# The first FFN's gating: GpSimd rounds three of four gate chunks, ScalarE scales a quarter of the sigmoids, and two loads are placed anew

## The chip, the cores and the metric

One core of a Trainium2 chip runs the whole program. The metric is the device time of one execution in microseconds (us), lower is better. The engines named here are TensorE (PE), VectorE (DVE), ScalarE (ACT), GpSimd (POOL) and SyncE (SP, which only issues DMAs); they run side by side and wait for each other by semaphores.

## The reference, cut to what matters

The program is a two-layer block over x of 16 x 256 tokens x 256 features: cross attention, a quantised gated FFN, a second cross attention, a butterfly FFN, each added to x through tanh of a gate. The change lies in the first FFN:

```python
def act_qdq(x):                        # one scale for the whole tensor
    qmax = 2.0 ** 15 - 1.0
    scale = jnp.maximum(jnp.max(jnp.abs(x)) / qmax, 1e-12)
    return jnp.clip(jnp.round(x / scale), -qmax - 1.0, qmax) * scale
...
x = act_qdq(x)                         # x is the normalised input
up = act_qdq(x @ lpbq_dequant(w_up).T)
gate = act_qdq(x @ lpbq_dequant(w_gate).T)
sig = fixed_qdq_u16(jax.nn.sigmoid(gate))    # rounded to multiples of 1/65536
gate = act_qdq(gate * sig)
o = act_qdq(gate * up)
return o @ lpbq_dequant(w_down).T
...
x = x + jnp.tanh(g_ffn[0]) * _L0_ffn_ref(_layernorm(x, axis=-1), ...)
```

Each `act_qdq` needs the maximum over all 4096 x 768 values before the first of them can be rounded. So the FFN falls into stages.

## The kernel before, in words

Everything is in `quantised_ffn` (L1463), built as three blocks one after another; in a block each engine runs its own list of instructions in order. Values lie as [128 partitions, batch pairs, 6 feature tiles (FT), tokens] in `hid`; `G` = 8 groups of 512 tokens, `GATES` = 48 tiles of 128x512.

**First block, gate products** (from 291.8 us of the span). VectorE computes x's scale, then `x_step` and `x_start` (L1667, L1668), and encodes and casts two of group 0's four tiles. ScalarE first waits for the gate value `g_in` and takes its tanh (L1788, L1789), then encodes the other two tiles and goes on to later groups (`encode`, `cast`, `turned`). TensorE transposes a group and multiplies it with the gate weights, in three passes per tile; ScalarE copies each tile to `hid` (L1808), and VectorE takes maxima and minima of two tiles at once (L1685). At the same time GpSimd composes the butterfly FFN's matrices from `low_paths` (L1847) and applies top stages to `w_con` (`top_stage`, L1556), using `ubuf` and `gcode` as room. SP's queue issues the load of `low_paths` first and that of `tg`, the gate value, second (L1857, L1858), then stores x's parts.

**First block, up products and gating** (from 385.1). TensorE multiplies with the up weights; for u = 0 to 47 ScalarE copies tile u to the ring `ubuf` of four (L1818), SP stores it to DRAM, and at every odd u VectorE takes the absolute maximum of two tiles (`up_max`, L1650; called R in the prediction). Among these, the gate values are treated in `NG` = 32 chunks of 128x768, placed by `CHUNKS_AT[i] = 3 + i*45//32`: chunk i is done after tile `CHUNKS_AT[i]`. For each chunk:
- `gate_code` (ScalarE, L1778): `gcode` = int16 of `hid` times the inverse scale, in a ring of three; waits until chunk i - 3 is `gated`;
- `sigmoid` (ScalarE, L1785): `sig` (ring of two) = sigmoid of `gcode` times the scale;
- `gate` (VectorE): `scode` = uint16 of `sig` x 65536 (L1655; S in the prediction), then `hid` = -(`gcode` x `scode`) with its maximum in `cmax` (L1659; T).

`gate_code(i + 1)` stands ahead of `sigmoid(i)` on ScalarE. From the second group on, TensorE also waits for x's parts, loaded back by SP (L1880). GpSimd has nothing to do here.

**Second block, multiplying back** (from 475.1; "stage three" in the change's name). After a second pair of scales, for 24 chunks of 128x1024: SP fetches the up values (`fetch_up`, three buffers), ScalarE rounds both factors (L1961, L1969), VectorE multiplies (L2006) and takes the maximum (L1991). Between the fetches SP issues the 1 MB loads of `blocks` (after fetch 5), `y` (7) and `z` (9), which TensorE multiplies from chunk 18 on (L1949) and in the third block. The third block (from 537.0) rounds the result, multiplies with the down weights and adds to x.

Within a block nothing but these lists and their semaphores orders the work; there is no planner.

Of the kernel before, what the change touches and what calls it, by code (L numbers as in the profile page):

```python
# [20 lines left out]
P = 128  # L21
# [1441 lines left out]
def quantised_ffn(nc, env, gate, butterfly):  # L1463
# [20 lines left out]
    with ctx:  # L1484
# [30 lines left out]
        def gate_part(i):  # L1515
            return flat[:, i * GW:(i + 1) * GW]
# [60 lines left out]
        with ExitStack() as ph:  # L1577
# [9 lines left out]
            xt_hi = tmp("xt_hi", [P, 2, DC, GT], F32R)  # L1587
            xt_lo = tmp("xt_lo", [P, 2, DC, GT], F32R)
            NU = 4
            GATES = G * FT  # L1590
            ubuf = tmp("ubuf", [P, NU, GT])
            gmax = tmp("gmax", [P, 2, GATES // 2])
            x_step = tmp("x_step", [P, NT])
            x_start = tmp("x_start", [P, NT])
            gcode = tmp("gcode", [P, 3, GW], I16)
            top = tmp("top", [P, 1])
            top_code = tmp("top_code", [P, 1], I16)
            top_sig = tmp("top_sig", [P, 1])
# [6 lines left out]
            gcoded, sig_ready, scoded, gated = (sem(x) for x in ("gcoded", "sig_ready", "scoded", "gated"))  # L1605
            topped, top_coded, top_sigged, top_scoded = (sem(x) for x in ("topped", "top_coded", "top_sigged", "top_scoded"))
            x_half = sem("x_half")
            paths_in, blocks_stored = sem("paths_in"), sem("blocks_stored")
            composed = [sem(f"composed{net}") for net in range(2)]
            g_in, x_max, x_all, x_scale = sem("g_in"), sem("x_max"), sem("x_all"), sem("x_scale")  # L1610
# [30 lines left out]
            def _(dve):  # L1641
# [9 lines left out]
                                      ALU.max, apply_absolute_value=True).then_inc(u_maxed, 1)  # L1651

                def gate(i):
                    dve.wait_ge(sig_ready, i + 1)
                    dve.tensor_scalar(scode[:, i % 2, :], sig[:, i % 2, :], 65536.0, None,  # L1655
                                      ALU.mult).then_inc(scoded, 1)
                    dve.wait_ge(scoded, i + 1)

                    dve.tensor_tensor_reduce(out=gate_part(i), in0=gcode[:, i % 3, :], in1=scode[:, i % 2, :],  # L1659
                                             scale=-1.0, scalar=0.0, op0=ALU.mult, op1=ALU.max,  # L1660
                                             accum_out=cmax[:, i:i + 1]).then_inc(gated, 1)

# [88 lines left out]
            @block.scalar  # L1751
            def _(act):
                def encode(g, tiles=GTT):
                    if g > 0:
                        act.wait_ge(x_float, g)
                    for t in range(tiles):
                        n = g * GTT + t
                        last = act.activation(xcode[:, t, :], xres[:, n, :], ACT.Identity, bias=x_start[:, n:n + 1],
                                              scale=x_step[:, n:n + 1])
                    last.then_inc(x_coded, 1)  # L1760

                def cast(g, tiles=GTT):
                    act.wait_ge(x_coded, g + 1)
                    if g > 0:
                        act.wait_ge(xt_ready, g * DC)
                    act.activation(xn[:, 0:tiles, :], xcode[:, 0:tiles, :], ACT.Copy).then_inc(x_float, 1)

                def turned(g):
                    if g >= 2:
                        act.wait_ge(x_saved[g % 2], 32 * (g // 2))  # L1770
                    for c in range(DC):
                        act.wait_ge(xt_ready, g * DC + c + 1)
                        act.activation(xt_hi[:, g % 2, c, :], (T0, T1)[c][:, :], ACT.Copy).then_inc(xt_rounded, 1)

                def gate_code(i):
                    if i >= 3:
                        act.wait_ge(gated, i - 2)
                    act.activation(gcode[:, i % 3, :], gate_part(i), ACT.Identity,  # L1778
                                   scale=codes[:, SG:SG + 1]).then_inc(gcoded, 1)

                def sigmoid(i):
                    act.wait_ge(gcoded, i + 1)
                    if i >= 2:
                        act.wait_ge(scoded, i - 1)
                    act.activation(sig[:, i % 2, :], gcode[:, i % 3, :], ACT.Sigmoid,  # L1785
                                   scale=scales[:, SG:SG + 1]).then_inc(sig_ready, 1)

                act.wait_ge(g_in, 16)  # L1788
                act.activation(tg[:], tg[:], ACT.Tanh)  # L1789
                act.wait_ge(x_scaled, 2)  # L1790
                encode(0, GTT // 2)
                cast(0, GTT // 2)
                act.wait_ge(x_half, 2)
                encode(1)
                turned(0)
                cast(1)
                for g in range(G):
                    for f in range(FT):
                        if f == 1 and g + 1 < G:
                            turned(g + 1)  # L1800
                        if f == 3 and g + 2 < G:
                            encode(g + 2)
                        if f == 4 and g + 2 < G:
                            cast(g + 2)
                        if g == PATH_GROUP and f == 0:
                            act.wait_ge(blocks_stored, 16)
                        act.wait_ge(prods, g * FT + f + 1)
                        act.activation(hid[:, 2 * g:2 * g + 2, f, :],  # L1808
                                       mm[(g * FT + f) % 6][:, :].rearrange("p (b t) -> p b t", t=T), ACT.Copy).then_inc(stored, 1)
                act.activation(warm[:], tg[:], ACT.Sigmoid)  # L1810
                act.wait_ge(z_sent, 16)
                for u in range(GATES):
                    m = GATES + u
                    act.wait_ge(prods, m + 1)
                    if u >= NU:
                        act.wait_ge(u_sent[u % NU], 16 * (u // NU))
                        act.wait_ge(u_maxed, (u - NU) // 2 + 1)
                    act.activation(ubuf[:, u % NU, :], mm[m % 6][:, :], ACT.Copy).then_inc(stored, 1)  # L1818
                    if u == FIRST_CHUNK - 1:
                        act.wait_ge(t_scale, 5)  # L1820
                        gate_code(0)
                    if u == FIRST_CHUNK + 1:
                        act.wait_ge(top_coded, 1)
                        act.activation(top_sig[:], top_code[:], ACT.Sigmoid,
                                       scale=scales[:, SG:SG + 1]).then_inc(top_sigged, 1)
                    for i in chunks_after(u):
                        if i + 1 < NG:
                            gate_code(i + 1)
                        sigmoid(i)

            @block.gpsimd
            def _(pool):
# [18 lines left out]
                for n, (q, i) in enumerate(stages):  # L1851
                    top_stage(pool, z_top[:, :, q * QW:(q + 1) * QW], z_parts[:, 0, :, :], z_parts[:, 1, :, :], 1, i,
                              z_mul, z_add, n)

            @block.sync
            def _(sp):
                sp.dma_start(paths, bf["low_paths"]).then_inc(paths_in, 16)  # L1857
                sp.dma_start(tg[:], gate).then_inc(g_in, 16)  # L1858
                for g in range(G - 2):
                    if g == PATH_GROUP - 2:  # L1860
                        for net in range(2):
# [37 lines left out]
        with ExitStack() as ph:  # L1899
# [19 lines left out]
            @block.sync  # L1919
            def _(sp):  # L1920
                def u_in(i):
                    before = i - NR
                    if before in DVE_CODES:
                        sp.wait_ge(u_coded, DVE_CODES.index(before) + 1)
                    else:
                        sp.wait_ge(ucoded, act_codes(before) + 1)
                    fetch_up(sp, i)

                for n in range(len(u_sent)):
                    sp.wait_ge(u_sent[n], 16 * GATES // len(u_sent))  # L1930
                for i in range(NR, NCH):
                    u_in(i)
                    if i == 5:
                        sp.dma_start(blocks[:].rearrange("p n t m -> p (n t m)"), bf["blocks_dram"]).then_inc(blocks_in, 16)
                    if i == 7:
                        sp.dma_start(y[:], bf["w_exp_t"].rearrange("(t p) d -> p t d", p=P)).then_inc(y_in, 16)
                    if i == 9:
                        sp.dma_start(z[:], bf["w2_dram"]).then_inc(z_in, 16)

            @block.tensor  # L1940
            def _(pe):
                pe.wait_ge(d_max, 1)
                spread_max(pe, 2, d_all)
                pe.wait_ge(blocks_in, 16)
                pe.wait_ge(y_in, 16)
                pe.wait_ge(multiplied, UNITS_FROM - 1)
                for n in range(HT // 2):
                    for t in range(2 * n, 2 * n + 2):
# [9 lines left out]
            def _(act):  # L1958
# [19 lines left out]

                for n in range(len(u_sent)):
                    act.wait_ge(u_sent[n], 16 * GATES // len(u_sent))  # L1980
                act.wait_ge(d_scale, 6)
                for i in range(NCH):
                    chunk(i)
# [39 lines left out]
        with ExitStack() as ph:  # L2023
# [331 lines left out]
            def _(pe):  # L2355
# [43 lines left out]

                pe.wait_ge(e_max, 1)  # L2400
                spread_max(pe, 1, e_all)
                pe.wait_ge(z_in, 16)
                for n in range(HT // 2):
                    if n == HT // 2 - 1:
                        pe.wait_ge(e_scale, 1)
# [457 lines left out]
```

## Time and profile before

| | us |
|---|---|
| median of 3 runs (lowest, highest) | 1094.6 (1093.14, 1094.95) |
| the profiled execution | 1098.77 |
| its span | 1097.0 |
| PE busy | 935.3 (85%) |
| DVE busy | 784.8 (72%) |
| ACT busy | 616.9 (56%) |
| POOL busy | 245.0 (22%) |
| first block, gate products | 291.8 to 385.1 of the span |
| first block, up products and gating | 385.1 to 475.1 |
| second block | 475.1 to 537.0 |

The times below are of the one profiled execution and count from the start of its span. Busy time is the time in which an engine ran at least one instruction; instructions that follow each other without a wait overlap by some 0.1 us, so the distance from start to start is a little less than a duration. A name such as `f_gcode<-f_hid,f_codes` reads output <- inputs. An idle time is followed by what ended it.

### The profile page before, as it was taken

What the parts mean: (1) busy time and instruction counts of PE and PEld (TensorE: products, weight loads), DVE (VectorE), ACT (ScalarE), POOL (GpSimd) and SP (SyncE); (2) the same over time, 40 slices, a digit from 0 to 9 for tenths busy, and PEclk for the clock granted to TensorE, in tenths of its full rate; (3) what the DMA queues carried; (4) which work ended last, traced back from release to release, by engine and by line L of the source; (5) the groups of instructions that cost most, each with busy time, mean ns of one, the idle gap of its engine ahead of it and who ended that gap; (6) DMA issues with size and microseconds to landing.
All of it is one profiled execution on the core that took longest, in us unless ns stands there. A gap on an engine that the chain in (4) does not pass through costs nothing. (4 is left out here: it accounts for less than half of the span.)

```text
span 1097.0 us, 20133 instructions
## 1 busy us (share of the span) xinstructions
PE 935.3 (85%) x6641; PEld 828.3 (76%) x6641; DVE 784.8 (72%) x1580; ACT 616.9 (56%) x1063; POOL 245.0 (22%) x436
## 2 busy tenths in 40 slices
PE   6589999999289998700699975999999998999998
PEld 5468888887168876500589964999999987998888
DVE  5358888876348889979889733777777768766671
ACT  4157777766167689969667434566666543222230
POOL 4223333321299000000022210111111104111210
PEclk9689999999679999955699986999999988999999
DMA  6845555541323167688222566755655510001001
GB/s 188 235 126 146 144 144 144 145 126 40 114 79 154 77 190 242 222 274 282 94 85 104 167 179 145 170 123 124 124 122 124 116 39 1 20 21 35 23 19 39
DMA packets 100356, 135.69 MB, mean 124 GB/s; under 512 B 42678, under 2 KB 76470, under 8 KB 97606
## 3 DMA queue, kind: packets, MB, share of 16 engines
q1 hardware_dynamic: 99382, 132.61, 42.9%
q10 hardware_dynamic: 608, 1.18, 0.5%
q0 software_dynamic: 304, 1.10, 0.3%
q8 instruction: 36, 0.59, 0.2%
q14 instruction: 26, 0.21, 0.1%
HBM read 69.73 MB, written 45.82 MB: 105 GB/s over the span
## 5 line engine op out<-in xcount | busy, mean ns | idle before, releaser
L2654 ACT ACTIVATE f_h<-bank,f_b 128x512 f32<-128x512 f32 x64 | 43.4, 691 | 112.9 <-PE bank L43 65.1
L41 PE MATMUL bank<-f_xt_hi,f_w_all 128*128 128x512 f32 x192 | 79.0, 412 | 9.7 <-DMA f_xt_lo<-x_spill 7.7
L685 DVE TENSOR_REDUCE a_maxima<-bank 128x4 f32<-128x308 f32 x128 | 60.3, 471 | 29.2 <-PE bank L769 27.8
L610 ACT ACTIVATE a_prob<-bank 77x512 f32<-77x512 f32 x128 | 72.3, 589 | 11.3 <-PE bank L794 10.9
L42 PE MATMUL bank<-f_xt_lo,f_w_all 128*128 128x512 f32 x192 | 77.4, 403 | 0.0
L43 PE MATMUL bank<-f_xt_hi,f_w_all 128*128 128x512 f32 x192 | 77.1, 402 | 0.0
L43 PE MATMUL bank<-f_w_hi,f_h_lo 128*128 128x256 f32 x256 | 72.4, 283 | 0.0
L42 PE MATMUL bank<-f_w_lo,f_h_hi 128*128 128x256 f32 x256 | 72.3, 282 | 0.0
L41 PE MATMUL bank<-f_w_hi,f_h_hi 128*128 128x256 f32 x256 | 72.0, 281 | 0.0
L791 PE MATMUL bank<-a_stack,a_kb 96*77 96x256 f32 x256 | 70.7, 300 | 0.6 <-ACT a_mt L603 0.5
L41 PE MATMUL bank<-f_d_hi,f_w_all 128*128 128x256 f32 (+1 forms) x224 | 64.6, 288 | 5.3 <-DVE f_w_all L2187 3.8
L1427 PE MATMUL bank<-a_values,a_prob 77*128 (+1 forms) x512 | 67.1, 275 | 0.0
L1685 DVE TENSOR_REDUCE f_gmax<-f_hid 128x1 f32<-128x1024 f32 x48 | 55.6, 1213 | 15.6 <-ACT f_hid L1808 15.6
L794 PE MATMUL bank<-a_mt,a_pick 128*77 128x256 f32 x256 | 66.1, 282 | 0.0
L42 PE MATMUL bank<-f_d_lo,f_w_all 128*128 128x256 f32 (+1 forms) x224 | 63.8, 285 | 0.0
L43 PE MATMUL bank<-f_d_hi,f_w_all 128*128 128x256 f32 (+1 forms) x224 | 63.8, 285 | 0.0
L1427 PEld LDWEIGHTS bank<-a_values,a_prob 77*128 77x128 f32 x512 | 62.8, 193 | 0.0
L41 PE MATMUL bank<-a_wo_hi,a_at_hi 128*128 128x256 f32 x192 | 58.8, 306 | 1.7 <-DVE a_at_lo L689 1.7
L769 PE MATMUL bank<-a_kb,a_stack 96*128 96x156 f32 x256 | 52.2, 287 | 8.3 <-DVE a_maxima L685 4.9
L42 PE MATMUL bank<-a_wo_lo,a_at_hi 128*128 128x256 f32 x192 | 55.5, 289 | 0.0
L43 PE MATMUL bank<-a_wo_hi,a_at_lo 128*128 128x256 f32 x192 | 55.4, 289 | 0.0
L791 PEld LDWEIGHTS bank<-a_stack,a_kb 96*77 96x77 f32 x256 | 37.6, 147 | 21.1 <-ACT a_prob L610 9.5
(317 smaller groups left out, 3129.1 us busy)
## 6 DMA issues: line engine op xcount, KB each, us to landing
u_spill<-f_ubuf SPq DMA_DIRECT2D x48, 256.0 KB, 2.4
f_w_all<-u_spill SPq DMA_DIRECT2D x24, 512.0 KB, 4.6
a_stack<-a_queries SPq DMA_DIRECT2D x16, 512.0 KB, 4.8
a_q_max<-a_q_hi SPq DMA_DIRECT2D x30, 256.0 KB, 4.4
a_kb<-a_key_spill SPq DMA_DIRECT2D x96, 77.0 KB, 2.6
xres<-in_x SPq DMA_DIRECT2D x16, 256.0 KB, 4.2
a_queries<-a_q_hi SPq DMA_DIRECT2D x16, 256.0 KB, 3.5
a_queries<-a_q_lo SPq DMA_DIRECT2D x16, 256.0 KB, 3.8
```

The lines of the kernel that those rows point to most:

```text
L41: nc.tensor.matmul(out, w_hi, m_hi, start=start, stop=False)
L42: nc.tensor.matmul(out, w_hi, m_lo, start=False, stop=False)
L43: return nc.tensor.matmul(out, w_lo, m_hi, start=False, stop=stop)
L610: act.activation(prob[0:S, n % 4, :, :].rearrange("p a b -> p (a b)"), (S0, S1)[n % 2][0:S, :], ACT.Exp, scale=SCALE).then_inc(probs, 1)
L685: dve.tensor_reduce(maxima[:, t, 4 * k:4 * k + 4], MX[:, 0:4 * SE].rearrange("p (h s) -> p h s", s=SE)[:, :, 0:S], AX.X, ALU.max).then_inc ...
L769: last = pe.matmul(MX[:, 2 * n * SE:2 * (n + 1) * SE], stack[0:ROWS, par, pair, t * P:(t + 1) * P], kb[0:ROWS, par, :, pair, :], start=Tru ...
L791: pe.matmul(out, kb[0:ROWS, par, a, pair, 0:S], stack[0:ROWS, par, pair, :], start=True, stop=False)
L794: last = pe.matmul(out, pick[:, 2 * pair + a, 0:S], mt[:, par, :], start=False, stop=True)
L1427: last = pe.matmul(out_of(t, h), prob[0:S, n % 2, a, t * P:(t + 1) * P], v, start=True, stop=True)
L1685: dve.tensor_reduce(gmax[:, side, m // 2:m // 2 + 1], hid[:, 2 * g:2 * g + 2, f - 1:f + 1, :], AX.XYZ, op).then_inc(g_maxed, 1)
L2654: act.activation(h[:, n % 2, :], hbank[n % 4][:, :], ACT.Gelu, bias=b1[:, n:n + 1]).then_inc(h_ready, 1)
```

## The change

- The rounding of chunk i to `gcode` stays on ScalarE for i = 0, 4, 8, ... (`ACT_CODES`) and is done by GpSimd for the other 24 chunks; `gcode` becomes a ring of four (`NC`).
- The scaling of the sigmoids to `scode` is done by ScalarE for i = 2, 6, 10, ... (`ACT_SIGMA`, 8 chunks), right behind the sigmoid, and stays on VectorE for the others.
- The tanh of the gate moves from the start of the first block to ScalarE's list in the second block; `tg` is loaded ahead of `low_paths`.
- `blocks`, `y` and `z` are loaded in halves after fetches 8, 10, 12, 14, 16 and 18.

```diff
+            NC = 4
+            ACT_CODES = list(range(0, NG, 4))
+            ACT_SIGMA = list(range(2, NG, 4))
+            def before(those, i):
+                return sum(n < i for n in those)
-            gcode = tmp("gcode", [P, 3, GW], I16)
+            gcode = tmp("gcode", [P, NC, GW], I16)
...
                 def gate(i):
-                    dve.wait_ge(sig_ready, i + 1)
-                    dve.tensor_scalar(scode[:, i % 2, :], sig[:, i % 2, :], 65536.0, None,
-                                      ALU.mult).then_inc(scoded, 1)
-                    dve.wait_ge(scoded, i + 1)
+                    if i in ACT_SIGMA:
+                        dve.wait_ge(act_scoded, ACT_SIGMA.index(i) + 1)
+                    else:
+                        dve.wait_ge(sig_ready, i + 1)
+                        if i >= 2:
+                            dve.wait_ge(gated, i - 1)
+                        dve.tensor_scalar(scode[:, i % 2, :], sig[:, i % 2, :], 65536.0, None,
+                                          ALU.mult).then_inc(scoded, 1)
+                        dve.wait_ge(scoded, i + 1 - before(ACT_SIGMA, i))
...
                 def gate_code(i):
-                    if i >= 3:
-                        act.wait_ge(gated, i - 2)
+                    if i not in ACT_CODES:
+                        return
+                    if i >= NC:
+                        act.wait_ge(gated, i + 1 - NC)
...
                 def sigmoid(i):
-                    act.wait_ge(gcoded, i + 1)
+                    if i in ACT_CODES:
+                        act.wait_ge(gcoded, ACT_CODES.index(i) + 1)
+                    else:
+                        act.wait_ge(pool_gcoded, i + 1 - before(ACT_CODES, i))
                     if i >= 2:
-                        act.wait_ge(scoded, i - 1)
+                        if i - 2 in ACT_SIGMA:
+                            act.wait_ge(act_scoded, ACT_SIGMA.index(i - 2) + 1)
+                        else:
+                            act.wait_ge(scoded, i - 1 - before(ACT_SIGMA, i - 2))
...
-                act.wait_ge(g_in, 16)
-                act.activation(tg[:], tg[:], ACT.Tanh)
+                    if i in ACT_SIGMA:
+                        act.wait_ge(sig_ready, i + 1)
+                        if i >= 2:
+                            act.wait_ge(gated, i - 1)
+                        act.activation(scode[:, i % 2, :], sig[:, i % 2, :], ACT.Copy,
+                                       scale=65536.0).then_inc(act_scoded, 1)
...
+                act.wait_ge(g_in, 16)
                 act.activation(warm[:], tg[:], ACT.Sigmoid)
...
+                pool.wait_ge(t_scale, 5)
+                for i in range(NG):
+                    if i in ACT_CODES:
+                        continue
+                    if i >= NC:
+                        pool.wait_ge(gated, i + 1 - NC)
+                    pool.tensor_scalar(gcode[:, i % NC, :], gate_part(i), codes[:, SG:SG + 1], None,
+                                       ALU.mult).then_inc(pool_gcoded, 1)
...
+                sp.dma_start(tg[:], gate).then_inc(g_in, 16)
                 sp.dma_start(paths, bf["low_paths"]).then_inc(paths_in, 16)
-                sp.dma_start(tg[:], gate).then_inc(g_in, 16)
...
-                    if i == 5:
-                        sp.dma_start(blocks[:]..., bf["blocks_dram"]).then_inc(blocks_in, 16)
-                    if i == 7:
-                        sp.dma_start(y[:], bf["w_exp_t"]...).then_inc(y_in, 16)
-                    if i == 9:
-                        sp.dma_start(z[:], bf["w2_dram"]).then_inc(z_in, 16)
+                    if i in (8, 10):      # half of blocks each
+                    if i in (12, 14):     # half of y each
+                    if i in (16, 18):     # half of z each
...
+                act.activation(tg[:], tg[:], ACT.Tanh)
                 act.wait_ge(d_scale, 6)
```

The last edit is in the second block; its and the third block's waits for `blocks`, `y` and `z` go from 16 to 32.

## Rows read from the trace of the kernel before

**Rows 1.** Busy time by window: from:to, us, busy us (instructions), clock, DMA share, GB/s.
```profile
291.80:385.10 93.30, 79.51 (x357) 64.70 (x358) 65.51 (x74) 57.00 (x103) 54.56 (x70) 0.88 0.32 125
385.10:475.10 90.00, 70.72 (x289) 54.23 (x287) 79.90 (x142) 79.41 (x116) 0.00 (x0) 0.94 0.71 227
475.10:537.00 61.90, 7.90 (x32) 6.72 (x32) 55.14 (x51) 52.91 (x53) 0.00 (x0) 0.53 0.70 231
```

The busy columns are PE, PEld, DVE, ACT, POOL.

**Rows 2.** Timeline, ScalarE at 302: start, us, instruction, idle before it.
```profile
302.16 0.20 ACT L1789 ACTIVATE f_tg<-f_tg 128x1 f32<-128x1 f32 x1 [12.24 <-DMA f_tg<-in_gf]
302.27 1.07 ACT L1758 ACTIVATE f_scode<-xres,f_x_start,f_x_step 128x256 int16<-128x256 f32 x2
```

**Rows 3.** DMA issues: KB each, us from issue to landing.
```profile
f_tg<-in_gf SPq DMA_DIRECT2D x1, 0.5 KB, 9.9
```

**Rows 4.** Timeline, VectorE at 294.
```profile
293.95 0.23 DVE L1668 TENSOR_SCALAR f_x_start<-nmr_all,f_codes 128x32 f32<-128x32 f32 x1
```

**Rows 5.** Timeline, the gating: VectorE's first, a middle and the last chunk, one ScalarE row.
```profile
393.22 0.56 DVE L1655 TENSOR_SCALAR f_scode<-f_sig 128x768 uint16<-128x768 f32 x1 [0.43 <-ACT f_sig L1785]
...
455.15 1.22 DVE L1650 TENSOR_REDUCE f_amax<-f_ubuf 128x2 f32<-128x1024 f32 x1
456.28 0.55 DVE L1655 TENSOR_SCALAR f_scode<-f_sig 128x768 uint16<-128x768 f32 x1
456.87 0.96 DVE L1659 CUSTOM_DVE_ANT_0 f_hid<-f_gcode,f_scode 128x768 f32<-128x768 int16 x1
457.75 0.08 DVE L1659 DVE_READ_ACCUMULATOR2_ANT f_cmax<- 128x1 f32 x1
...
457.87 0.94 ACT L1778 ACTIVATE f_gcode<-f_hid,f_codes 128x768 int16<-128x768 f32 x1 [0.37 <-DVE f_cmax L1659]
...
472.05 0.08 DVE L1659 DVE_READ_ACCUMULATOR2_ANT f_cmax<- 128x1 f32 x1
```

**Rows 6.** Waits from 485 to 505 (us, times, longest); busy time from 486 to 496.
```profile
ACT f_ucode L1961 <- DMA f_w_all<-u_spill: 4.7, 4, 1.6
DVE f_hid L2006 <- ACT f_g2code L1969: 3.1, 4, 1.5
...
486.00:496.00 10.00, 0.00 (x0) 0.00 (x0) 8.06 (x8) 6.45 (x6) 0.00 (x0) 0.50 1.01 371
```

**Rows 7.** Busy time from 355 to 385; line L1685: ns min/median/max, first and last start.
```profile
355.00:385.00 30.00, 30.00 (x138) 24.39 (x137) 26.61 (x26) 18.50 (x33) 0.13 (x1) 1.00 0.18 70
...
L1685 DVE TENSOR_REDUCE f_gmax<-f_hid x48: 1206/1210/1222, 315.5 to 386.3; 128x1 f32<-128x1024 f32 x48
```

**Rows 8.** Timeline, ScalarE at the start of the second block.
```profile
475.45 1.15 ACT L1961 ACTIVATE f_ucode<-f_w_all,f_codes 128x1024 int16<-128x1024 f32 x1 [6.41 <-DVE f_minus L2000]
```

**Rows 9.** Groups by line, ScalarE, 385 to 475: busy us, mean ns, idle before.
```profile
L1778 ACT ACTIVATE f_gcode<-f_hid,f_codes 128x768 int16<-128x768 f32 x32 | 29.8, 931 | 2.5 <-DVE f_cmax L1659 1.4
```

**Rows 10.** GpSimd's nearest forms: min/median/max of the memset; groups of two others.
```profile
L280 POOL MEMSET a_kb<- x1: 2183/2183/2183, 4.5 to 4.5; 128x2496 f32 x1
...
L1560 POOL TENSOR_TENSOR f_gcode<-f_ubuf,f_top_coef 128x512 f32<-128x512 f32 x12 | 12.5, 1046 | 0.9
L1573 POOL TENSOR_TENSOR f_ubuf<-f_gcode 128x512 f32<-128x512 f32 x12 | 15.5, 1296 | 0.9
```

**Rows 11.** Timeline, third block: two GpSimd adds (merged), VectorE beside and after them.
```profile
569.97 6.28 POOL L2082 TENSOR_TENSOR f_y<-f_y,f_y_pair 128x1028 f32<-128x1028 f32 x2 [25.33 <-ACT f_y L2316]
...
571.30 2.69 DVE L2187 TENSOR_TENSOR f_w_all<-f_ocode,f_w_all 128x1536 fp32r<-128x1536 int16 x1 [0.72 <-ACT f_w_all L2263]
574.03 3.13 DVE L2182 TENSOR_SCALAR f_ocode<-f_hid,f_codes 128x1536 int16<-128x1536 f32 x1
...
579.00 1.74 DVE L2187 TENSOR_TENSOR f_w_all<-f_ocode,f_w_all 128x1536 fp32r<-128x1536 int16 x1
580.78 1.02 DVE L2182 TENSOR_SCALAR f_ocode<-f_hid,f_codes 128x1536 int16<-128x1536 f32 x1
```

**Rows 12.** Waits from 385 to 475, TensorE for x loaded back.
```profile
PE bank L41 <- DMA f_xt_lo<-x_spill: 7.7, 6, 2.0
```

More of the change, by code:

```diff
@@ L1607, in quantised_ffn @@
             x_half = sem("x_half")
+            pool_gcoded, act_scoded = sem("pool_gcoded"), sem("act_scoded")
             paths_in, blocks_stored = sem("paths_in"), sem("blocks_stored")
@@ L1653, in gate @@
                 def gate(i):
-                    dve.wait_ge(sig_ready, i + 1)
-                    dve.tensor_scalar(scode[:, i % 2, :], sig[:, i % 2, :], 65536.0, None,
-                                      ALU.mult).then_inc(scoded, 1)
-                    dve.wait_ge(scoded, i + 1)
-                    dve.tensor_tensor_reduce(out=gate_part(i), in0=gcode[:, i % 3, :], in1=scode[:, i % 2, :],
+                    if i in ACT_SIGMA:
[7 more added lines that the diff above has]
+                        dve.wait_ge(scoded, i + 1 - before(ACT_SIGMA, i))
+                    dve.tensor_tensor_reduce(out=gate_part(i), in0=gcode[:, i % NC, :], in1=scode[:, i % 2, :],
                                              scale=-1.0, scalar=0.0, op0=ALU.mult, op1=ALU.max,
@@ L1775, in gate_code @@
                 def gate_code(i):
-                    if i >= 3:
-                        act.wait_ge(gated, i - 2)
-                    act.activation(gcode[:, i % 3, :], gate_part(i), ACT.Identity,
+                    if i not in ACT_CODES:
+                        return
+                    if i >= NC:
+                        act.wait_ge(gated, i + 1 - NC)
+                    act.activation(gcode[:, i % NC, :], gate_part(i), ACT.Identity,
                                    scale=codes[:, SG:SG + 1]).then_inc(gcoded, 1)
                 def sigmoid(i):
-                    act.wait_ge(gcoded, i + 1)
+                    if i in ACT_CODES:
+                        act.wait_ge(gcoded, ACT_CODES.index(i) + 1)
+                    else:
+                        act.wait_ge(pool_gcoded, i + 1 - before(ACT_CODES, i))
                     if i >= 2:
-                        act.wait_ge(scoded, i - 1)
-                    act.activation(sig[:, i % 2, :], gcode[:, i % 3, :], ACT.Sigmoid,
-                                   scale=scales[:, SG:SG + 1]).then_inc(sig_ready, 1)
-                act.wait_ge(g_in, 16)
-                act.activation(tg[:], tg[:], ACT.Tanh)
+                        if i - 2 in ACT_SIGMA:
+                            act.wait_ge(act_scoded, ACT_SIGMA.index(i - 2) + 1)
+                        else:
+                            act.wait_ge(scoded, i - 1 - before(ACT_SIGMA, i - 2))
+                    act.activation(sig[:, i % 2, :], gcode[:, i % NC, :], ACT.Sigmoid,
+                                   scale=scales[:, SG:SG + 1]).then_inc(sig_ready, 1)
+                    if i in ACT_SIGMA:
[4 more added lines that the diff above has]
+                                       scale=65536.0).then_inc(act_scoded, 1)
                 act.wait_ge(x_scaled, 2)
@@ L1932, in _ @@
                     u_in(i)
-                    if i == 5:
-                        sp.dma_start(blocks[:].rearrange("p n t m -> p (n t m)"), bf["blocks_dram"]).then_inc(blocks_in, 16)
-                    if i == 7:
-                        sp.dma_start(y[:], bf["w_exp_t"].rearrange("(t p) d -> p t d", p=P)).then_inc(y_in, 16)
-                    if i == 9:
-                        sp.dma_start(z[:], bf["w2_dram"]).then_inc(z_in, 16)
+                    if i in (8, 10):
+                        net = (i - 8) // 2
+                        sp.dma_start(blocks[:, net, :, :].rearrange("p t m -> p (t m)"),
+                                     bf["blocks_dram"][:, net * HID1:(net + 1) * HID1]).then_inc(blocks_in, 16)
+                    if i in (12, 14):
+                        half = slice((i - 12) // 2 * HT // 2, ((i - 12) // 2 + 1) * HT // 2)
+                        sp.dma_start(y[:, half, :], bf["w_exp_t"].rearrange("(t p) d -> p t d", p=P)[:, half, :],
+                                     ).then_inc(y_in, 16)
+                    if i in (16, 18):
+                        half = slice((i - 16) // 2 * HT // 2, ((i - 16) // 2 + 1) * HT // 2)
+                        sp.dma_start(z[:, half, :], bf["w2_dram"][:, half, :]).then_inc(z_in, 16)
             @block.tensor
@@ L1943, in _ @@
                 spread_max(pe, 2, d_all)
-                pe.wait_ge(blocks_in, 16)
-                pe.wait_ge(y_in, 16)
+                pe.wait_ge(blocks_in, 32)
+                pe.wait_ge(y_in, 32)
                 pe.wait_ge(multiplied, UNITS_FROM - 1)
@@ L2401, in _ @@
                 spread_max(pe, 1, e_all)
-                pe.wait_ge(z_in, 16)
+                pe.wait_ge(z_in, 32)
                 for n in range(HT // 2):
```

## The prediction

> **What bounds the kernel now.** I read the page's busy shares first (table of the profile section), then busy time by window, because the change touches three neighbouring stretches with different limits [rows 1]: the gate products of the first FFN (291.8 to 385.1 us of the span), the up products beside the gating (385.1 to 475.1) and the multiplying back (475.1 to 537.0). TensorE leads the kernel as a whole, but none of the three edits shortens TensorE's work; each window has to be read by itself.
>
> In the first window the timeline of ScalarE shows 12.24 us of idle before its first instruction, the tanh of the gate, and the DMA that brings the one gate value as what ended it [rows 2]. That DMA carries 0.5 KB and took 9.9 us, being issued after the 2 MB of `low_paths` on the same queue [rows 3]. The encoding of x stands behind the tanh. Its own input, `x_start`, was there at 293.95 + 0.23 = 294.18 [rows 4]. From then on the stretch runs at TensorE's pace.
>
> In the second window ScalarE has 79.4 us and VectorE 79.9 us of work in 90.0, both more than TensorE's 70.7 [rows 1]. VectorE does for a chunk S (scale the sigmoids, L1655), T (multiply and maximum, L1659), and for every second up tile R (maximum, L1650). From start to start [rows 5]: R takes 456.28 - 455.15 = 1.13, S 0.59, T 0.88. From S of chunk 0 to the end of T of chunk 31 the row pair gives 472.13 - 393.22 = 78.9. Its work in that time: 22 R after that first S (one per two up tiles from tile 5 on, by the code) x 1.13 = 24.9, and 32 x 1.47 = 47.0, together 71.9. The other 7.0 are waits for ScalarE, which in turn waits for a free `gcode` buffer, as in the row at 457.87 [rows 5]. So the two engines hold each other up, and TensorE is ahead of both.
>
> In the third window VectorE has 55.1 us in 61.9 [rows 1], and ScalarE feeds it. Between 485 and 505 it waited 3.1 us for ScalarE, which waited 4.7 us for the fetched up values; there the DMA share is 1.01 [rows 6]: the three 1 MB loads, put between fetches 5, 7 and 9, take the room.
>
> **Part 1, the tanh moved and the gate loaded first: -8.0 us.** ScalarE can encode at about 294.25 instead of 302.27 [rows 2, 4], 8.0 earlier. VectorE's half of the tiles is done by 295.4 and would not be waited for much longer than before. What else is asked of this stretch: `low_paths` is issued one issue later on SP's queue; GpSimd's chain behind it has one instruction left after 355 [rows 7], its result is stored from there, and ScalarE needs that store at 385 - 8 = 377, so the cover is some 20 us. The first x stores now meet the tail of the `w_con` load; nobody waits for them until the third group. The tanh itself (0.20) goes to the third stage, where ScalarE idles 6.41 before its first code [rows 8]; if that were uncovered it would cost 0.2. It has to be on SP's queue before anything waits, and it is. I take -8.0, bounds -7 to -8.5, for the clock: its mean in this window is 0.88 of 2.4 GHz [rows 1], and a shorter gap can move its rise either way.
>
> **Part 2, the gating. What goes.** ScalarE loses 24 of 32 codes, 24 x 0.93 = 22.3, and gains 8 scalings to uint16; no such row, the nearest is the code's form at 0.93 [rows 9], so 7.4, and some 0.1 each for the wait on its own sigmoid. Its 79.4 become about 65: no longer a limit. VectorE loses 8 S. Its work becomes 24.9 + 24 x 1.47 + 8 x 0.88 = 67.2.
>
> **What comes: 24 GpSimd instructions of 128x768, D each.** The trace has no tensor-scalar on GpSimd. Below: a memset of 2496 in 2.18, so 0.67 for 768. Above: a multiply with a second operand, 512 in 1.046, so 1.57; an add of two full tensors, 1.296, so 1.94 [rows 10]. An instruction with one tensor read and one write lies between the first two; I take their middle, D = 1.1, and keep 0.67, 1.57 and 1.94. GpSimd is idle in this window, so 24 D = 26 fits easily; D matters for what it holds.
>
> It holds VectorE. [Rows 11] show a GpSimd add running from 569.97 to 576.25 in two pieces. VectorE's tensor-scalar L2182, float32 to int16 and of S's kind, takes 1.02 alone and 3.13 beside it, ending 0.91 after GpSimd's end; L2187, which like T reads two SBUF tensors, takes 2.69 where it began beside the first piece, against 1.74 alone. Whoever comes second waits for the whole of the other. R reads one tensor and isn't held: 48 like it beside or after GpSimd's chain in the first window all took the same 1.21 [rows 7].
>
> When does GpSimd come? Chunk i waits for T of chunk i - 4, so it starts about 0.16 after that T's successor has begun (accumulator row at 457.75 + 0.08, and another engine released by it starts at 457.87 [rows 5]; rounded up). Three are done at the start; 21 remain. In 14 cases R follows that T: R covers 1.13, and VectorE loses D + 0.16 - 1.13 = D - 0.97 when that is positive (nothing otherwise). In 7 cases (chunks 1, 5, 11, 15, 18, 21, 25, where the schedule puts two chunks on neighbouring tiles) S or T follows at once, GpSimd gets in behind it, and VectorE loses the whole D. With D = 1.1: 14 x 0.13 + 7 x 1.1 = 9.5. Then 67.2 + 9.5 + 1.0 of remaining waits for ScalarE (an estimate, between 0 and the 7.0 of now) = 77.7 against 78.9, and the first sigmoid comes 0.5 earlier, since no code stands ahead of it: **-1.7**. With D = 0.67 the loss is 4.7 and the part -6.5; with 1.57 it is 19.4 and the part +8.2; with 1.94, 27.2 and +16.0.
>
> The Trainium skill, "GPSIMD Engine Reference" (Engine selection), says that one-input elementwise work on GpSimd is roughly at line rate; at 1.03 cycles of 1.2 GHz it would be an estimate of 0.66 us, the lower end, and the part would be -6.5. No row here has that form. "SBUF — State Buffer" (Who interferes with whom) states the lock and extends it to every VectorE instruction with two SBUF inputs; whether T's custom form obeys it no row here shows. If it does, the sum above stands; if it doesn't, it is the first rival.
>
> **Part 3, the loads in halves: -2.5 us.** Six halves at fetches 8 to 18 instead of three wholes at 5 to 9. VectorE's pace is 55.1 / 24 = 2.3 per chunk, so 12 chunks are 27.6 us in which 6.3 MB of up values and 3.1 MB of halves must come: 341 GB/s against 371 moved in the crowded window [rows 6]. The 3.1 us of waits can go; I keep 0.6. The bounds are 0 and -3.1. TensorE asks for blocks and y after chunk 17, and the last half of y is issued when code 11 is done; z is asked for in the stage after.
>
> **Sum.** -8.0 - 1.7 - 2.5 = -12.2. The profiled execution took 1098.77 (span 1097.0), so it would be 1086.6; it stands 4.2 above the median of the runs, and the same difference taken from 1094.6 gives 1082.4.
>
> **The rivals.** (a) GpSimd hardly holds T: VectorE's loss falls to about 2 us, the gating to 70.2, or -9.2 with the start. Against more: TensorE's work of 70.7 plus waits for x_back, 7.7 now [rows 12]. Total -19.7: 1074.9. For it: T's form is not in the trace beside GpSimd. Against it: L2187 is.
> (b) GpSimd rounds slowly but not very, D = 1.3 to 1.6: the second part gives back +3 to +9, the total is -8 to -2: about 1090. For it: every GpSimd row with arithmetic takes 1.57 or more per 768.
> (c) Slower than before: one mechanism, the lock between GpSimd's rounding and S and T. The other parts and the earlier start are -11.0; VectorE's work and its remaining 1.0 are 10.7 under 78.9; so the loss 21 D - 13.6 must exceed 21.7, from D = 1.68 on. At the add's 1.94 the total is +5.5: 1100.1.
> (d) The earlier start doesn't come through (another wait takes its place, such as the z store or the x stores): -4.2 remains, 1090.4.
>
> **Chances.** The forecast (D 0.7 to 1.3, T held, total -8 to -17) 0.58, its own range 1078 to 1087; (a) 0.16; (b) 0.13; (c) 0.08; (d) 0.05. A measurement of this kernel tells about 0.2% from no change, 2.2 us. From that: faster 0.88, same 0.04 (the slow end of b), slower 0.08. The range 1072 to 1092 takes in (a), (d) and most of (b).
>
> **What would show it.** Right: ScalarE's encoding starts near 294.3; the window of the gate products keeps its length from there; S and T have members of 1.5 to 2.2 us beside L1655's 0.55 and L1659's 0.96, and R none; VectorE has hardly any idle time in the gating, ScalarE much; no wait for fetched up values between 485 and 505 of the old clock. Wrong: GpSimd's instructions under 0.8 or over 1.4; T's maximum at 0.96; R waiting for ScalarE as now; waits for y or blocks ahead of L1949; a table load at the moved tanh (1.28, beside 6.41 of idle).

## The result, and the profile after

| | before | after |
|---|---|---|
| median us (lowest, highest, runs) | 1094.66 (1093.14, 1094.95, 4) | 1082.93 (1081.58, 1083.81, 4) |
| the profiled execution, its span | 1098.77, 1097.0 | 1083.48, 1081.5 |

The ratio is 0.988, 95% interval [0.9856, 0.9903]: 10.6 to 15.8 us less, 11.7 between the medians. Forecast were 12.2 less. Measured again in a later series (`i13_again` below), the same kernel gave 0.9841 [0.9812, 0.987] (1078.94 against 1095.39), which is 14.2 to 20.6 us less. Both intervals lie clear of 1; the forecast lies inside the first and 2 us short of the second.

Busy time of the three stretches after, as [rows 1] has them before (from:to, us, busy us of PE, PEld, DVE, ACT, POOL, clock, DMA share, GB/s):

```profile
290.42:375.21 84.79, 79.00 (x357) 64.35 (x358) 65.53 (x74) 56.91 (x103) 54.64 (x70) 0.92 0.36 137
375.21:460.93 85.72, 70.43 (x289) 54.24 (x287) 79.31 (x136) 66.88 (x100) 58.77 (x24) 0.94 0.74 239
460.93:522.96 62.03, 7.24 (x32) 6.25 (x32) 55.41 (x50) 52.89 (x53) 0.00 (x0) 0.56 0.70 229
```

The first is 8.5 us shorter, the second 4.3, the third the same within 0.1. VectorE's 79.31 didn't fall although 8 S are gone; ScalarE's fell by 12.5; GpSimd has 58.77, more than twice the 26 that the prediction gave it.

The start, VectorE and ScalarE (timeline; idle before and what ended it), against [rows 2, 4]:

```profile
292.59 0.23 DVE L1682 TENSOR_SCALAR f_x_start<-nmr_all,f_codes 128x32 f32<-128x32 f32 x1
...
292.86 1.09 ACT L1772 ACTIVATE f_scode<-xres,f_x_start,f_x_step 128x256 int16<-128x256 f32 x2 [4.30 <-DVE f_x_start L1682]
```

The encoding now begins 0.04 after `x_start` and no longer 8.09 after it. (The whole trace lies 1.36 us earlier at this point; that is from ahead of the change.)

The gating: GpSimd's rounding, S, T (ns min/median/max, first and last start), then the groups of T, R, S and ScalarE's scaling (busy us, mean ns, idle before):

```profile
L1887 POOL TENSOR_SCALAR f_gcode<-f_hid,f_codes x24: 2198/2426/3060, 379.5 to 449.4; 128x768 int16<-128x768 f32 x24
L1669 DVE TENSOR_SCALAR f_scode<-f_sig x24: 543/552/1140, 382.8 to 456.2; 128x768 uint16<-128x768 f32 x24
L1673 DVE CUSTOM_DVE_ANT_0 f_hid<-f_gcode,f_scode x32: 949/959/1543, 383.4 to 456.8; 128x768 f32<-128x768 int16 x32
...
L1673 DVE CUSTOM_DVE_ANT_0 f_hid<-f_gcode,f_scode 128x768 f32<-128x768 int16 x32 | 33.2, 1047 | 0.8
L1659 DVE TENSOR_REDUCE f_amax<-f_ubuf 128x2 f32<-128x1024 f32 x24 | 29.2, 1215 | 3.7 <-ACT f_ubuf L1845 3.5
L1669 DVE TENSOR_SCALAR f_scode<-f_sig 128x768 uint16<-128x768 f32 x24 | 14.7, 612 | 0.0
L1813 ACT ACTIVATE f_scode<-f_sig 128x768 uint16<-128x768 f32 x8 | 6.8, 845 | 1.0 <-DVE f_cmax L1673 0.6
```

GpSimd's instruction takes 2.2 us at least, above every bound of the prediction. Yet T loses only (1.047 - 0.959) x 32 = 2.8 us to it and S (0.612 - 0.552) x 24 = 1.4, together 4.2. R stays at 1.22. Two places of the timeline show why:

```profile
406.86 1.21 DVE L1659 TENSOR_REDUCE f_amax<-f_ubuf 128x2 f32<-128x1024 f32 x1
407.04 4.39 POOL L1887 TENSOR_SCALAR f_gcode<-f_hid,f_codes 128x768 int16<-128x768 f32 x2 [1.68 <-DVE f_cmax L1673]
407.99 0.95 DVE L1673 CUSTOM_DVE_ANT_0 f_hid<-f_gcode,f_scode 128x768 f32<-128x768 int16 x1
...
410.79 0.96 DVE L1673 CUSTOM_DVE_ANT_0 f_hid<-f_gcode,f_scode 128x768 f32<-128x768 int16 x1
411.67 0.08 DVE L1673 DVE_READ_ACCUMULATOR2_ANT f_cmax<- 128x1 f32 x1
411.67 0.56 DVE L1669 TENSOR_SCALAR f_scode<-f_sig 128x768 uint16<-128x768 f32 x1
411.85 2.45 POOL L1887 TENSOR_SCALAR f_gcode<-f_hid,f_codes 128x768 int16<-128x768 f32 x1 [0.42 <-DVE f_cmax L1673]
412.26 1.54 DVE L1673 CUSTOM_DVE_ANT_0 f_hid<-f_gcode,f_scode 128x768 f32<-128x768 int16 x1
```

GpSimd works from 407.04 to 411.43 without a gap, two instructions of 2.2 us. The two T that begin in that time, 0.95 after the start of the first and 1.57 after that of the second, take their usual 0.96. At 411.85 GpSimd begins while S runs, and takes 0.25 more than its 2.20. T, which follows S, is then 0.58 longer, so it began in effect at 412.84, with 1.46 us of GpSimd's 2.45 still to come. Only the first part of GpSimd's instruction holds T.

### The profile page after: what moved, and what is told of

Its sections match the earlier page's. It is cut to its first block and busy times, and to the rows that moved or that the text cites. A ratio compares the mean times of both kernels' runs of the same rounds, so it can differ in the third digit from the quotient of the medians.

```text
span 1081.5 us, 20168 instructions
## 1 busy us (share of the span) xinstructions
PE 929.9 (86%) x6641; PEld 824.8 (76%) x6641; DVE 783.9 (72%) x1572; ACT 604.1 (56%) x1047; POOL 303.3 (28%) x460
## 5 line engine op out<-in xcount | busy, mean ns | idle before, releaser
L41 PE MATMUL bank<-f_xt_hi,f_w_all 128*128 128x512 f32 x192 | 78.7, 410 | 6.8 <-DMA f_xt_lo<-x_spill 4.6
L685 DVE TENSOR_REDUCE a_maxima<-bank 128x4 f32<-128x308 f32 x128 | 60.3, 471 | 27.8 <-PE bank L769 26.3
L1887 POOL TENSOR_SCALAR f_gcode<-f_hid,f_codes 128x768 int16<-128x768 f32 x24 | 58.8, 2460 | 37.9 <-DVE f_codes L1553 24.6
L42 PE MATMUL bank<-f_d_lo,f_w_all 128*128 128x256 f32 (+1 forms) x224 | 63.9, 285 | 0.0
```

Source lines behind the costliest of these rows:

```text
L41: nc.tensor.matmul(out, w_hi, m_hi, start=start, stop=False)
L42: nc.tensor.matmul(out, w_hi, m_lo, start=False, stop=False)
L685: dve.tensor_reduce(maxima[:, t, 4 * k:4 * k + 4], MX[:, 0:4 * SE].rearrange("p (h s) -> p h s", s=SE)[:, :, 0:S], AX.X, ALU.max).then_inc ...
L1887: pool.tensor_scalar(gcode[:, i % NC, :], gate_part(i), codes[:, SG:SG + 1], None, ALU.mult).then_inc(pool_gcoded, 1)
```

## Experiments

Two durations recur below. "The gating" is from the start of the first S to the end of the last T, 78.9 before and 75.0 after. "The second block" is from the reciprocal L1551 of its scales to the next block's, 63.75 before and 64.04 after. Both are of one profiled execution each.

### One part at a time

`f1_tanh`: only the tanh and the order of the two loads.

```diff
-                act.wait_ge(g_in, 16)
-                act.activation(tg[:], tg[:], ACT.Tanh)     # ahead of encode(0)
+                act.activation(tg[:], tg[:], ACT.Tanh)     # second block, ahead of d_scale
```

> Part 1 alone: the gate value loaded first, its tanh in the second block. The theory that the early start passes through whole says -8.0 to -8.6 us (the encoding starts 8.06 earlier than before once both are counted from x_start, and the gate products then took another 0.5 less): 1086 to 1087. The rival that the saved time is partly taken by a wait behind it, such as the z store or the x stores, says -5 or less.

Measured: 1087.2, ratio 0.9927 [0.9907, 0.9947], 8.0 us less (5.8 to 10.2). From the first reciprocal to the table load at the end of the gate products it took 83.2 us. Over all traces: 83.1 on average in the ten that have this part, 91.0 in the four that don't. That is 7.9 us, and the time fell by as much; the rival, 5 us or less, lies outside the interval.

`f2_gate`: the rings, GpSimd's loop and `ACT_SIGMA` of the diff alone.

> Part 2 alone: GpSimd rounds 24 chunks, ScalarE scales 8 sigmoids. The gating of the changed kernel took 75.0 us from the first S to the last T against 78.9, and 4.4 less in all; if this is part 2's own, the kernel takes -4 us: 1090 to 1091. If it is the work of the earlier start (another clock, other DMA traffic), about 0 to -2, as the prediction had it at -1.7.

Measured: 1090.73, ratio 0.9963 [0.9942, 0.9983], 4.1 us less (1.9 to 6.3); gating 74.75, as in the changed kernel. Part 2's gain is its own: it came without the earlier start.

`f3_halves` and `f4_no_halves`: the loads in halves alone, and everything but that.

> Part 3 alone: the three 1 MB loads as six halves at fetches 8 to 18. The prediction's step says -2.5 us (1092.1), VectorE's waits between 485 and 505 going from 3.1 to 0.6. The theory from the trace after says about 0 (-0.5 to +1): the halves move the waits to the last third of the second block, where ScalarE has the unit copies too (2.56 us a chunk against VectorE's 2.27) and can't catch up.

> The changed kernel with its third part undone (whole loads after fetches 5, 7 and 9). By the prediction's step it takes 2.5 us more than the changed kernel: 1085.4. By the theory from the trace after it takes the same or up to 1 us less: 1082 to 1083.

Measured: 1094.72, ratio 0.9993 [0.9971, 1.0015], and 1084.84, ratio 0.9896 [0.9856, 0.9936]. Neither tells the third part from nothing. The second block took 62.49 with the halves alone and 63.82 in `f4_no_halves`. In seven traces with halves it took 61.3 to 64.0, 62.3 on average; in five with whole loads 63.65 to 64.4, 63.9. So by the traces the halves are worth some 1.6 us, and the first profile of the changed kernel was the worst of the seven. "About 0", my reading of that one trace, does not stand, and the step's 2.5 is more than this average gives; the times alone exclude neither.

### What GpSimd holds

`g5_forms`: the kernel before, with work of no use on GpSimd after each gated chunk; the outputs stay the same.

```diff
+                for i in range(NG):
+                    pool.wait_ge(gated, i + 1)
+                    if i % 4 == 0: ...pool.memset(probe[:], 0.0), three times
+                    if i % 4 == 1: pool.tensor_scalar(probe, gate_part(i), codes[...], None, ALU.mult)
+                    if i % 4 == 2: pool.tensor_tensor(probe, gate_part(i), gate_part(i), ALU.add)
+                    if i % 4 == 3: pool.tensor_scalar(probe_code, gate_part(i), ...)   # int16
```

> The kernel before, with GpSimd doing work of no use beside the gating: after chunk i is gated, for i mod 4 = 0 three memsets of 128x768, for 1 a tensor-scalar float32 to float32, for 2 an add of two tensors, for 3 a tensor-scalar float32 to int16 (the changed kernel's form). Nothing of the result changes. Theory of two phases: GpSimd's reading holds VectorE's S and T, its writing holds S alone, and between them it holds nothing; so T stays at 0.96 beside the memsets and only S grows, while T grows by up to about 0.75 beside the reading forms, never by their whole length. Rival, the prediction's: the whole instruction holds both, so T grows beside the memsets too, and by up to 2.2 beside the int16 form. Price: if the conversion is what makes 2.2 us, the float32 form takes 1.0 to 1.5; if any tensor-scalar with a scalar from memory does, it takes 2.2 as well.

One run: 1108.25, against 1095.82 for the kernel before beside it; gating 87.9. GpSimd's groups there (busy us, mean ns), then the timeline at three places:

```profile
L1865 POOL MEMSET f_probe<- 128x768 f32 x24 | 19.9, 830 | 41.7 <-DVE f_cmax L1662 40.6
L1869 POOL TENSOR_SCALAR f_probe<-f_hid,f_codes 128x768 f32<-128x768 f32 x8 | 18.8, 2353 | 3.8 <-DVE f_cmax L1662 3.3 <-POOL f_probe L1865 0.5
L1873 POOL TENSOR_SCALAR f_probe<-f_hid,f_codes 128x768 int16<-128x768 f32 x8 | 18.1, 2266 | 11.5 <-DVE f_cmax L1662 11.5
L1871 POOL TENSOR_TENSOR f_probe<-f_hid 128x768 f32<-128x768 f32 x8 | 12.0, 1498 | 1.4 <-DVE f_cmax L1662 0.6
```

```profile
400.63 1.47 POOL L1871 TENSOR_TENSOR f_probe<-f_hid 128x768 f32<-128x768 f32 x1
401.04 1.48 DVE L1658 TENSOR_SCALAR f_scode<-f_sig 128x768 uint16<-128x768 f32 x1
...
417.37 1.09 POOL L1865 MEMSET f_probe<- 128x768 f32 x1 [0.35 <-DVE f_cmax L1662]
417.81 0.96 DVE L1662 CUSTOM_DVE_ANT_0 f_hid<-f_gcode,f_scode 128x768 f32<-128x768 int16 x1
...
444.61 1.72 POOL L1871 TENSOR_TENSOR f_probe<-f_hid 128x768 f32<-128x768 f32 x1 [0.37 <-DVE f_cmax L1662]
445.03 2.11 DVE L1662 CUSTOM_DVE_ANT_0 f_hid<-f_gcode,f_scode 128x768 f32<-128x768 int16 x1
```

The price: the tensor-scalar takes 2.2 to 2.45 whatever it writes. The add of the same size takes 1.47 in seven of eight rows (1.72 where S stood in its way, hence the mean of 1.50); it reads one tensor twice and lies below the 1.94 that the prediction scaled from another add of [rows 10]. The conversion isn't what costs.

The hold: T that begins beside a memset keeps its 0.96 (it begins at 417.81, the memset runs from 417.37 to 418.46), while S beside a memset reaches 1.16. Beside the add T is 1.15 longer and begins in effect at 446.18, 0.15 before the add's end; S, too, waits to within 0.15 of the add's end. Beside either tensor-scalar T grows by at most 0.58. So the prediction's whole-instruction hold is true of the add, which [rows 11] had shown, and false of the form that the change uses.

Where the tensor-scalar holds can be read from the changed kernel's own trace:

```profile
425.76 4.68 POOL L1887 TENSOR_SCALAR f_gcode<-f_hid,f_codes 128x768 int16<-128x768 f32 x2 [2.21 <-DVE f_cmax L1673]
...
427.59 0.79 DVE L1669 TENSOR_SCALAR f_scode<-f_sig 128x768 uint16<-128x768 f32 x1
```

This S ends at 428.38 and so began in effect at 427.83, 2.07 after GpSimd's start. Take every T and S that was lengthened, count from GpSimd's start, and take off what GpSimd itself had been delayed (its duration less 2.20). Five T and three S then begin in effect at 0.75 to 0.76, four S at 2.06, 0.14 before GpSimd's end. A T that begins at 0.95 or later is never lengthened, nor is an S between 0.77 and 0.98. It works the other way too: where an S ends 1.67, 1.94 or 2.38 after GpSimd's start, GpSimd takes 2.34, 2.62 or 3.06, each time 0.68 more than that; taken from 2.20 this gives 1.52. So the instruction holds both T and S up to 0.75, then nothing, then S alone from about 1.5 to 2.06. This bears out the theory of phases. That the first phase is its reading and the second its writing is inferred, from the memset, which only writes and holds only S.

### What sets the gating's pace

`g6_no_sigma` and `g7_sigma15`: `ACT_SIGMA` emptied, and made every second chunk.

```diff
-            ACT_SIGMA = list(range(2, NG, 4))
+            ACT_SIGMA = []                       # g6; g7: list(range(2, NG, 2))
```

> The changed kernel with all 32 sigmoid scalings back on VectorE; GpSimd still rounds 24 chunks. VectorE's work is again 71.9 us plus what GpSimd holds (4 to 6, S being the form that is held most), so first S to last T takes 77 to 79 instead of 75.0, and the kernel 1085 to 1087. If ScalarE's lightening was what helped, and VectorE's 8 scalings do not matter, it stays at 75 and 1083.

> The changed kernel with every second sigmoid scaling on ScalarE (chunks 2, 4, ... 30; 15 instead of 8). VectorE's work falls by another 4.1 us and its held S are fewer; ScalarE's comes to some 66. If VectorE is what still sets the pace, first S to last T takes 71 to 72.5 and the kernel 1079.5 to 1081, TensorE's pace (about 71) being next. If the coupling over the two sig buffers is, it stays at 74 to 75 and 1082 to 1083.

Measured: `g6_no_sigma` 1084.36, ratio 0.9897 [0.9875, 0.992], gating 77.9, which is in the expected span (the time is 0.6 below its own). `g7_sigma15` 1081.85, ratio 0.9868 [0.9842, 0.9894], gating 73.5, 1 us above the expected span, as is the time. Both intervals overlap with the change's [0.9856, 0.9903], so the order of the three rests on the traces. In the first, sigmoids wait 11.9 us for S, in the second R waits 5.7 for the up tiles (waits: us, times, longest):

```profile
ACT f_sig L1807 <- DVE f_scode L1669: 11.9, 14, 1.9
```

```profile
DVE f_amax L1659 <- ACT f_ubuf L1845: 5.7, 9, 2.0
```

`i9_sigma_only` and `i14_all_gpsimd`: no chunk rounded by GpSimd, and 31 of them (one run each).

```diff
-            ACT_CODES = list(range(0, NG, 4))
+            ACT_CODES = list(range(NG))          # i9; i14: [0]
```

> The changed kernel with all codes on ScalarE, so GpSimd does nothing in the gating and ScalarE still scales 8 sigmoids. ScalarE's work is then 79.4 + 7 us: first S to last T takes 82 to 86, longer than before the change (78.9), and 7 to 11 us longer than the changed kernel's. If it stays at 75 to 78, it was ScalarE's help to VectorE, not GpSimd's to ScalarE, that brought the gain.

> The changed kernel with 31 of 32 codes on GpSimd. At 2.2 to 2.6 us each (2.46 on average in the changed kernel) they take 68 to 76 us one after the other, so GpSimd itself comes to set the pace: first S to last T 76 to 79, sigmoids waiting for GpSimd's codes. If GpSimd's length stays without effect, 74 to 75, ScalarE having 6 us less to do.

Measured: gating 81.8 (a fifth of a us under the expected span; 1091.47), and 77.6 (1085.63). In the latter:

```profile
ACT f_sig L1807 <- POOL f_gcode L1887: 10.7, 16, 1.3
```

So the gating takes 78.9 with neither help; 81.8 with ScalarE's help to VectorE alone; 77.9 with GpSimd's help to ScalarE alone; 74.6 with both, on average (five traces). Busy time from the first S to the last T says why. Before, ScalarE had 73.2 and VectorE 71.9. With the scalings alone ScalarE, the first limit, has 78.7 of the 81.8. With GpSimd alone ScalarE falls to 55.4, but VectorE rises to 76.5 of the 77.9: its 71.9 and 4.6 in which GpSimd holds it. With both VectorE has 71.2 and ScalarE 60.9. So GpSimd alone brings 1 us, the scalings alone cost 3, and together they bring 4.3.

With 31 chunks GpSimd is busy for 72.8 of the 77.6, and sigmoids wait 10.7 for it; VectorE is held longer as well (74.6 busy). How much of the 3.0 us each of the two costs isn't separated. The ring of four was not tried by itself either; in the trace before ScalarE waited 1.4 us for a free `gcode` buffer, which bounds what a fourth buffer could have saved it there.

### The loads in smaller pieces, and both variations together

`g8_quarters`: twelve loads of 256 KB after fetches 8 to 19. `i10_both`: that and 15 scalings. `i13_again`: the changed kernel once more beside it.

```diff
-                    if i in (8, 10): ...half of blocks;  (12, 14): half of y;  (16, 18): half of z
+                    if 8 <= i < 12: ...quarter of blocks;  12 to 15: quarter of y;  16 to 19: quarter of z
```

> The changed kernel with blocks, y and z in twelve 256 KB pieces, one after each of fetches 8 to 19. Theory: a fetch is issued when ScalarE has read the buffer three chunks before, 5.8 us ahead of need, and lands in 4.6 to 5.6; a 512 KB piece ahead of it takes 1.4 us of the queue's bandwidth and makes it late, a 256 KB piece 0.7 and hardly. Then the waits for fetched values fall from 5.1 to 1 or less, the second block is 1.5 to 3 us shorter, and the kernel takes 1080 to 1081.5. Rival: what counts is the sum of bytes in the late part of the block, so the waits stay (4 to 5 us) and the time too (1083).

> The changed kernel with both of the earlier variations: 15 sigmoid scalings on ScalarE and the loads in twelve 256 KB pieces. If the two gains seen in the traces (first S to last T 73.5 instead of 75.0; second block 60.6 instead of some 62.5) are real and add, it takes 2 to 4 us less than the changed kernel on the same chip, about 1079 to 1081. If they are differences between single executions, it is within 1 us of it.

> The changed kernel itself once more, beside the others on the same chip: 1082 to 1084, and a second profile of it. If the 64.0 us of its second block in the first profile were a single execution's, it now shows 61.3 to 62.5, as the other kernels with the same loads did; if they belong to the kernel, 64 again.

Measured: `g8_quarters` 1082.92, ratio 0.987 [0.9846, 0.9895]; second block 60.55, waits for fetched values 1.9. The block is as short as expected, but 1.9 is more than the 1 expected, and the time misses the 1080 to 1081.5. `i13_again` 1078.94, ratio 0.9841, 3 us below the expected 1082; second block 62.47, waits 3.9, so the 64.0 were a single execution's. `i10_both` 1078.83, ratio 0.9834 [0.9808, 0.9859]; gating 73.2, second block 60.3. Its wait row beside that of the changed kernel's first profile:

```profile
ACT f_ucode L2003 <- DMA f_w_all<-u_spill: 0.4, 1, 0.4
```

```profile
ACT f_ucode L2001 <- DMA f_w_all<-u_spill: 5.1, 6, 1.7
```

In the windows concerned `i10_both` is 1.4 + 2.2 us shorter than `i13_again`, and both gains are those of `g7_sigma15` and `g8_quarters` again, so they recur. But the medians differ by 0.1, with intervals of 0.25% either way; the expected 2 to 4 us did not show. The profiled execution of `i10_both` took 4.2 us more behind the second block's end (557.3 against 553.1), a stretch of 553.1 to 558.6 in the eleven traces with neither variation and of 557.3 to 559.0 in the three with one or both. That it is faster than the change isn't shown, and a loss elsewhere that takes it back isn't either.

## Why the prediction was right

The time and the sign were right. One of the steps beneath was wrong twice over, with errors that cancelled, so that the total came out so near is in part luck.

- **Part 1, -8.0**: 8.0 measured alone, 7.9 between the traces. The stretch moved as a whole, and no table load came at the moved tanh.
- **Part 2, -1.7**: 4.1 measured alone. The first sigmoid came the forecast 0.5 earlier (7.58 from the table load to the first S, 8.09 before). ScalarE and VectorE were rightly named as the two limits, but the `gcode` buffer by which the prediction ties them together was worth 1.4 us of waits; VectorE waited 5.9 for ScalarE's copies of the up tiles. The failed step is "VectorE loses the whole D". D was taken as 1.1, with 1.94 as its highest bound, and is 2.2 to 2.45: the form with one tensor input isn't cheaper than the ones with two there. Put into the prediction's own formula, 2.2 would have cost 21 x 2.2 - 13.6 = 32.6 us and made rival (c) of it, slower by some 11. But the hold is not D: T waited 0.58 in 5 of 32 cases, S 0.59 once and 0.1 to 0.24 in five, 4.2 in all against the 9.5 of the sum. The remaining waits took part of that back, 3.6 instead of 1.0: 67.2 + 4.2 + 3.6 = 75.0, where 77.7 was forecast.
- **Part 3, -2.5**: about -1.6 in the second block, not separable in time. VectorE's 3.1 us of waits in the window named did fall, to 0.5 in the first profile, but over the whole block they are 6.3 against 6.4: others came later. ScalarE waited for fetched values six times (5.1, 3.9 and 3.6 us in three traces) instead of four times for 4.7. With 256 KB pieces, and the same bytes, two traces show 1.9 and 0.4 of waits and a block 3.5 shorter than with whole loads. So the sum of bytes, on which the step rests, is not what failed; that a 512 KB piece makes the fetch behind it late fits this and is inferred.
- **The rivals**: the forecast's own condition, D of 0.7 to 1.3, did not hold, and no rival had named what came: a long D with a short hold. (a) has the better mechanism, T being held for a part only. It named a loss of 2 and a gating of 70.2; the loss was 4.2, and waits 2.6 longer than its 1.0 took the rest of the 4.8 that it is off. (b) and (d) fall. (c) fell through the hold, not through D.
- **Its marks**: S and T "of 1.5 to 2.2" came true for T at 1.54 and not for S (1.14 at most). "GpSimd over 1.4" was named as a sign of a wrong step, and it was one. "No wait for fetched up values" between 485 and 505 did not come true: 2.9 us in two waits at the same place (471 to 491 after).

By the traces' averages the parts add up to -7.9 - 0.5 - 4.3 - 1.6 = -14.3, between the two measurements (-13.1 and -17.4 by the ratios), so 12.2 was perhaps 2 us short.

## What to carry to other kernels

Where two engines exclude each other, the price of work moved to one of them isn't its duration but the part of it in which it holds what the other needs; look for that part by setting a long instruction's row beside those that overlap it. When two engines are about equally loaded, look what relieving one does to the other: GpSimd's help alone was worth 1 us, because it took 18 us from ScalarE but cost VectorE 4.6, ScalarE's help alone was a loss of 3, and both together brought 4.3. Where no row has the form itself, bound its duration more widely than by its neighbours: here the simpler form was the dearer.

## What the runs showed of the hardware

- GpSimd's tensor-scalar of 128x768 with a per-partition scalar takes 2.2 us where nothing delays it, to float32 or int16; an add of the same size, one tensor read twice, 1.47, a memset 0.74 (`g5_forms`).
- Beside GpSimd's add, VectorE's two-input T and its one-input S both wait to within 0.15 us of the add's end. Beside a memset only S waits. Beside the tensor-scalar T and S wait up to 0.75 us from its start, and S again from about 1.5 to 2.06. R, a one-input reduction, is never held (1.21 to 1.22). The Trainium skill, "SBUF — State Buffer" (Who interferes with whom), says that a two-input VectorE instruction contends with GpSimd's reads and not with an instruction that only writes; the memset rows agree (T at 0.96 from 417.81, the memset from 417.37 to 418.46), and T's custom form obeys it too. Its statement that GpSimd keeps the pair for its whole instruction agrees with the add (2.11 at 445.03) and not with the tensor-scalar, where two T at 0.96 began inside 4.39 us of GpSimd's work: there the measurement decides.
- "GPSIMD Engine Reference" of the Trainium skill (Engine selection) calls one-input work roughly line-rate; the tensor-scalar here took 2.2 us, over three times the 0.66 estimated from that page, so this form doesn't bear it out.
